# Batch 2's projections ahead of batch 0's values, and batch 3's row statistics on ScalarE

## The reference, cut to what matters

```
x [4,512,512], ctx [4,512,256]
q = ctx @ Wq.T + bq ; k = ctx @ Wk.T + bk          # [512,128] each
attention = softmax(q @ k.T, axis=-1)              # [512,512]
x1 = x + layernorm(x) @ attention.T                # x_m[l,m] = sum_n ln(x)[l,n] attention[m,n]
v  = layernorm(x1)
h  = bf16(layernorm(bf16(v)) * ln_w + ln_b)
h  = bf16(quant(h) @ quant(W1).T + b1)             # quant: 8 bits, one exponent for 32 values
h  = bf16(gelu(h))
h  = bf16(quant(h) @ quant(W2).T + b2)
out = x1 + bf16(bf16(v) + h)
```

## Time and profile before

| what | value |
|---|---|
| median of 3 runs | 273.33 us (271.74 to 273.48) |
| the profiled execution's own time | 274.33 us |
| its span, first to last instruction | 272.5 us |
| mean granted TensorE clock | 0.948 of full speed |
| DVE busy | 243.0 us, 89% of the span |
| PE busy | 226.3 us, 83% |
| ACT busy | 175.7 us, 64% |
| POOL busy | 68.1 us, 25% |
| DMA | 42.92 MB, mean 157 GB/s |

### The profile page before, as it was taken

One profiled execution on the slowest core, in us unless ns is written; L12 is line 12 of the kernel. 1 busy time (PEld: TensorE's weight loads), 2 busy tenths in 40 slices (PEclk: granted clock), 3 DMA queues, 4 the chain that ended last, 5 costly groups with the idle time before them and its releaser, 6 DMA issues.

```text
span 272.5 us, 3187 instructions
## 1 busy us (share of the span) xinstructions
PE 226.3 (83%) x931; PEld 97.5 (36%) x940; DVE 243.0 (89%) x354; ACT 175.7 (64%) x303; POOL 68.1 (25%) x101
## 2 busy tenths in 40 slices
PE   6774859989995937559996797899999789999993
PEld 6432314434431413214442333344444234444431
DVE  3599964999999999999979999999999999877982
ACT  2377753669997739767789798855556554556510
POOL 2193200042007300160521200633203333333400
PEclk9996868999999986968999999999999999999999
DMA  5999999999899828693060522656650566655773
GB/s 153 373 400 291 247 163 265 285 224 224 161 262 224 165 40 219 128 195 78 0 117 0 96 49 50 110 122 135 135 132 20 119 135 140 135 129 118 157 183 123
DMA packets 103078, 42.92 MB, mean 157 GB/s; under 512 B 93845, under 2 KB 96153, under 8 KB 102553
## 3 DMA queue, kind: packets, MB, share of 16 engines
q1 hardware_dynamic: 100224, 36.45, 61.0%
q10 hardware_dynamic: 2360, 6.30, 7.5%
q0 software_dynamic: 480, 0.02, 0.1%
HBM read 15.48 MB, written 4.19 MB: 72 GB/s over the span
## 4 chain that ended last, share of the span: by engine, by line
DVE 50%; PE 24%; DMA 10%; ACT 7%; issue 3%; SPq 3%; POOL 2%; ACTq 0%; DVEq 0%; POOLq 0%
DVE amax L862 12%; PE ps L821 9%; PE ps L811 5%; PE ps L758 5%; DMA pT<-phl 4%; DVE pf L976 4%; DVE wquant L966 4%; DVE w_int L905 3%; DVE phl L1047 3%; DMA xhl<-pf 3%; DVE vw L1059 3%; DVE hq L1064 3%; DVE xhl L1052 3%; DVE wquant L971 2%; DVE nmax L1033 2%
## 5 line engine op out<-in xcount | busy, mean ns | idle before, releaser
L821 PE MATMUL ps<-w2T,xhl 128*128 128x512 bf16 x247 | 56.5, 379 | 8.3 <-DMA xhl<-pf 7.9
L811 PE MATMUL ps<-w1T,cxT 128*128 128x512 bf16 x256 | 58.0, 380 | 0.0
L641 ACT ACTIVATE wst<-ps 128x1024 bf16<-128x1024 f32 x32 | 32.0, 1017 | 24.3 <-PE ps L811 24.3
L862 DVE TENSOR_REDUCE amax<-phl 128x64 f32<-128x2048 bf16 x16 | 36.5, 2281 | 4.0 <-ACT phl L648 4.0
L821 PEld LDWEIGHTS ps<-w2T,xhl 128*128 128x128 bf16 x256 | 24.4, 98 | 39.0 <-DMA xhl<-pf 8.3
L811 PEld LDWEIGHTS ps<-w1T,cxT 128*128 128x128 bf16 x256 | 23.7, 98 | 32.6 <-issue 6.2
L758 PE MATMUL ps<-h1q,xT 128*128 128x512 f16 x96 | 26.5, 435 | 9.8 <-ACT xs L546 6.2
L648 ACT ACTIVATE phl<-wst 128x2048 bf16<-128x2048 bf16 x16 | 30.6, 1910 | 1.6 <-DVE wquant L966 0.5
L758 PE MATMUL ps<-pT,xT 128*128 128x512 f16 x96 | 24.5, 410 | 7.5 <-DMA pT<-phl 7.0
L471 POOL TENSOR_TENSOR wst<-wst,vs 128x512 bf16<-128x512 bf16 x12 | 15.3, 1275 | 53.2 <-DVE wquant L971 53.2
L506 ACT ACTIVATE pf<-ps,nmax 128x512 f32<-128x512 f32 x16 | 10.8, 678 | 19.5 <-DVE nmax L1033 19.4
(11 more groups left out here) (90 smaller groups left out, 370.6 us busy)
## 6 DMA issues: line engine op xcount, KB each, us to landing
wst<-in_L_ffn_W ACTq DMA_DIRECT2D x6, 1024.0 KB, 6.5
xs<-in_x SPq DMA_DIRECT2D x4, 1024.0 KB, 8.0
out_x<-wst SPq DMA_DIRECT2D x16, 256.0 KB, 2.9
cx<-in_ctx SPq DMA_DIRECT2D x4, 512.0 KB, 5.7
wst<-in_L_ffn_W SPq DMA_DIRECT2D x2, 1024.0 KB, 11.3
xhl<-pf SPq DMA_TRANSPOSE x17, 4.3
lnw<-in_L_ffn_ln_w SPq DMA_DIRECT2D x1, 256.0 KB, 12.6
lnb<-in_L_ffn_ln_b SPq DMA_DIRECT2D x1, 256.0 KB, 12.2
```

Source lines behind the costliest of these rows:

```text
L641: act.activation(ys[:, k, 1024 * g:1024 * g + 1024], ps_y[:, 2 * g:2 * g + 2, :], ACT.Copy)\
L811: last = pe.matmul(ps_y[:, c, :], h1T[:, k, t, :], w1T[:, 4 * c:4 * c + 4, t, :], start=False, stop=(t == KT - 1))
L821: last = pe.matmul(ps_z[:, k, :], h2T[:, k, t, :], w2T[:, t, :], start=False, stop=(t == FT - 1))
L862: dve.tensor_reduce(amax[:, a, :], by_block, AX_X, ALU.max, apply_absolute_value=True)\
```

## The change

Five edits:

1. **SP**: the loads of `lnw` and `lnb` move from before `load_ctx(2)` to behind `front(1, 3)`, and the wait for them on DVE moves from before `front(2, ...)` to behind it, just before their first use in `back(2, 2, 0)`.
2. **PE**: a new `first_batches()` has 22 small matmuls on the identity behind `energies(0,3)` (their result is never read); `context(2)` moves before `energies(1,0)`; `queries_keys(2)` and `energies(1,2)` move ahead of `values(0,0)`; `energies(1,3)` moves before `values(0,1)`; `energies(2,0)` and `(2,1)` move in among batch 0's values.
3. **ACT**: `context(2)` moves into the first batch; `exp(1,1)`, `x_high(1,1)` and `p_high(1,0)` move ahead of batch 2's four `x_square`; `query_key(2,0)` and `(2,1)` move ahead of `p_high(1,3)`, with a wait for `energies(1,3)`, since they overwrite `qkT`.
4. **ACT, DVE and POOL**: batch 3's statistics move from DVE (`x_stats(3)` is gone) to ACT: 4 `x_sum` between `load_w1(2)` and `x_plus(0,3)`, 4 `x_square` behind `x1_square(0,3)`. POOL gets `mean_x(3)` ahead of `mean_x1(0)` and `factors_x_summed(3)` in place of `factors_x(3)`.
5. The bookkeeping counts of `st` and `mvr` lose their `min(b, 2)`.

```diff
             sp.dma_start(wst[:, W2, :], w2_t[0]).then_inc(ld_w2, 16)
-            sp.dma_start(lnw[:, :], ln_w.rearrange("(o n) -> o n", o=1).broadcast_to([P, H])).then_inc(ld_ln, 16)
-            sp.dma_start(lnb[:, :], ln_b.rearrange("(o n) -> o n", o=1).broadcast_to([P, H])).then_inc(ld_ln, 16)
             load_ctx(2)
             front(0)
             load_x(3)
             front(1, 3)
+            sp.dma_start(lnw[:, :], ln_w.rearrange("(o n) -> o n", o=1).broadcast_to([P, H])).then_inc(ld_ln, 16)
+            sp.dma_start(lnb[:, :], ln_b.rearrange("(o n) -> o n", o=1).broadcast_to([P, H])).then_inc(ld_ln, 16)
             front(2)
...
             def batch(b, x, v):
+                if b == 0:
+                    mean_x(3)
                 mean_x1(b)
                 if v is not None:
                     factors_v(v)
-                if x == 2:
+                if x is not None:
                     factors_x_summed(x)
-                elif x is not None:
-                    factors_x(x)
                 factors_x1(b)
...
+            def first_batch():
...
+                act.wait_ge(w_first, 1)
+                load_w1(1)
+                x_sum(2, 0)
+                x_sum(2, 1)
+                query_key(1, 0)
+                x_sum(2, 2)
+                query_key(1, 1)
+                context(2)
+                x_sum(2, 3)
+                exp(1, 0)
+                x_high(1, 0)
+                exp(1, 1)
+                x_high(1, 1)
+                p_high(1, 0)
+                for t in range(LT):
+                    x_square(2, t)
...
+                    if b == 0 and t == 3:
+                        act.wait_ge(e_ps, 2 * NT)
+                        query_key(2, 0)
+                        query_key(2, 1)
+                    if b > 0 and qk is not None and t == 3:
                         context(qk)
-                if front + 1 < B and b is not None:
+                if front + 1 < B:
                     load_w1(front + 1)
...
+                if b == 0:
+                    for t in range(LT):
+                        x_sum(3, t)
+                x_plus(b, LT - 1)
...
+                x1_square(b, 3)
+                if b == 0:
+                    for t in range(LT):
+                        x_square(3, t)
...
+            def first_batches():
+
+                energies(0, 2)
+                energies(0, 3)
+                keep_busy(22)
+                queries_keys(1)
+                context(2)
+                energies(1, 0)
+                energies(1, 1)
+                queries_keys(2)
+                energies(1, 2)
+                values(0, 0)
+                energies(1, 3)
+                values(0, 1)
+                values(0, 2)
+                energies(2, 0)
+                values(0, 3)
+                energies(2, 1)
...
             front(1, 1, 0, None, None)
             back(1, 1, None)
+            front(2, 2, 1, None, None)
             dve.wait_ge(ld_ln, 32)
-            front(2, 2, 1, 3, None)
             back(2, 2, 0)
```

More of the change, by code:

```diff
@@ L573, in v_sums @@
                                accum_out=sums[:, 1, 0, t:t + 1]).then_inc(v_sum, 1)
+            def first_batch():
+                for t in range(LT + 1):
+                    if t < NT:
+                        exp(0, t)
+                        x_high(0, t)
+                    if t > 0:
+                        p_high(0, t - 1)
+                    if t == 3:
+                        context(1)
+                act.wait_ge(w_first, 1)
[14 more added lines that the diff above has]
+                    x_square(2, t)
             def batch(b, front, qk, v):
                 for t in range(LT + 1):
-                    if t < NT and (t > 0 or front == 0):
+                    if t < NT and t > int(b == 0):
                         exp(front, t)
                         x_high(front, t)
-                    if t > 0:
+                    if t > int(b == 0):
                         p_high(front, t - 1)
-                    if b is not None and t > 1:
+                    if t > 1:
                         x_plus(b, t - 2)
@@ L630, in _ @@
             query_key(0, 1)
-            batch(None, 0, 1, None)
+            first_batch()
             batch(0, 1, 2, None)
@@ L764, in batch @@
             def batch(b, front, qk):
-                if qk is not None and b is not None:
+                if qk is not None:
                     context(qk)
                 for t in range(LT):
-                    if b == 0:
-                        values(b, t)
                     if t < NT - 2:
                         energies(front, t + 2)
-                    if b is not None and b > 0:
-                        values(b, t)
+                    values(b, t)
                 if qk is not None:
```

37 lines of the change are left out of this document (9 added, 28 removed).

## The result

| | before | after |
|---|---|---|
| median | 273.26 us (4 runs, 271.74 to 273.48) | 284.17 us (4 runs, 279.75 to 285.27) |
| the profiled execution, its span | 274.33, 272.5 us | 284.52, 282.7 us |
| DVE busy, and not busy, in the span | 243.0, 29.5 us | 240.2, 42.5 us |

The ratio is 1.0324, interval [1.0182, 1.0466]: slower by over 1 per cent, where 269.2 us and "faster" were forecast. The span grew by 10.2 us: DVE has 2.8 us less to do (the statistics have gone) and is idle for 13.0 us more.

A forecast was written before the change was run, and what follows sets the result against it. DVE, busy 243.0 of 272.5 us, was taken as the bound, with a 5.2 us stall on PE and ACT full behind it. 5.9 - 3.4 + 1.6 = 4.1 us less than 273.33 gave 269.2 us, range 267.3 to 271.5.

The forecast's parts named there:

- the sum: Whole kernel: 5.9 (stall gone) - 3.4 (ACT's added work) + 1.6 (statistics off DVE) = 4.1 us less.
- The paragraph on the clock: PE at full clock for `values(0,0)`, at half from about 56 us; `values(1,0)` then takes 6.1 us instead of 3.5.
- Rival E: Slower, up to 275.1 us, if crowded DMA engines start `values(0,0)` after 39.8 us at half clock; chance 0.05.
- Part 1: DVE's 5.2 us wait for `energies(1,2)` from PE goes; `negmax(1,2)` comes 5.9 us earlier, at 38.6.
- Part 2: ACT's longer row after `load_w1(2)` brings `exp(2,1)` only 2.5 us earlier; 3.4 of the 5.9 us are given back.
- Part 3: DVE drops `x_stats(3)`, 2.66 us, of which 1.6 count; `negmax(3,0)` starts 4.1 us earlier, at 83.05.
- rival B: Late transposes and half clock delay PE's `values(1,0)`, and with it `negmax(3,0)`: 3.0 us less, 270.3 us; chance 0.15.
- Rival C: Half clock at PE's `values(0,0)` makes `energies(1,3)` 1.5 us late: 2.6 us less, 270.7 us; chance 0.07.

The follow-up runs named there:

- x and context early: The changed kernel with batch 3's loads of x and context issued behind batch 0's transposes and ahead of W1's, `load_w2(1)` left in ACT's ring: 270.81 us.
- the two kernels with 1 MB more: The kernel before plus a spare 1 MB load that nobody reads, issued by ACT or by SP: 286.1 and 285.25 us.
- order only: The change without edits 4 and 5, so batch 3's statistics stay on DVE: 280.7 us (272.7 to 285.3).

## Why the prediction was wrong

**The step that failed** is not in the sum but in what the sum assumed: that each transfer lands as long after its issue as before. The paragraph on the clock says "now issued at 51.6, so 58.4 if the DMA engines keep up". Rival E says of crowding that "Nothing in the change adds to them before that", and was given 0.05 and at most 1.8 us; it looks only at the time before `values(0,0)`, and the crawl begins behind it, at 47 us. Both look at how much is moved; no byte was added, and the time between issues was what changed. The prediction moved `load_w1(2)` forward and has no line on `load_w2(1)`, which went 5.8 us forward among SP's loads and transposes. The runs show in its place: `load_w2(1)` landed in 19.0 us instead of 6.8 and the transposes in 20.0 to 24.0, DVE waited 14.3 us for weights, and the kernel came out 10.9 us slower; with that overlap taken out (273.38), or with the crawl absent for another reason (270.4 to 270.8), the loss is gone.

The Trainium skill (DMA: Bandwidth & Descriptors, Rules for kernel authors) says that a "transpose next to ordinary DMAs needs nothing". That row is about wrong results, and of time it says nothing. For the time it isn't so here: with one transpose beside a load, each took 15.5 us, instead of 3 to 8.

The rest can be judged on the change with x and context early, which is the change without the crawl:

| step | forecast | there |
|---|---|---|
| Part 1, `negmax(1,2)`, `negmax(1,3)` | 38.6, 43.0 | 38.48, 42.87 |
| Part 2, `load_w1(2)`, `exp(2,1)` | 50.8, 61.6 | 50.67, 61.61 |
| Part 2, `p_low(2,0)` | 63.6 | 63.63 |
| clock, `values(1,0)` at half clock | from 58.4 | from 61.30, 5.04 us for its 12 matmuls |
| Part 3, `negmax(3,0)` | 83.05 | 83.78, waits 1.57 for PE |
| the sum | 4.1 us | 3.3 us of span, 3.5 us of median |

- **Part 1 was right** in time and in mechanism. Its small matmuls were not needed: without them `queries_keys(1)` runs at half clock, and DVE's `negmax(1,2)` is no later.
- **Part 2 was right** to 0.1 us. The 3.4 us that ACT pays are the statistics: without these, `exp(2,1)` comes at 57.86 in the kernel with x and context early, 3.75 us before the 61.61.
- **Part 3 was 0.7 us too hopeful**, for rival B's reason. Its 1.6 us of gain stand beside a cost of 3.4 in Part 2 that belongs to the same move, so by the prediction's own terms the statistics lose 1.8 us and should have stayed on DVE. The runs show 0 to 2 us lost in the new order and 4.0 in the old, where 2.66 us of DVE's work went and 5.8 us of waits came.
- **Rival B came in** inside the kernel without the crawl: `values(1,0)` late and at half clock, `negmax(3,0)` 3.3 us early, 3.0 forecast. That its 3.3 us of span also lie near the forecast's 4.1 is no merit of the forecast, whose transposes land at 58.4.
- **Rival C didn't**: `values(0,0)` ran at full clock, 2.75 us. The granted clock fell later: in the changed kernel it is 1.00 up to 57 us and 0.50 from 58 on, with PE idle since the end of `context(3)`'s transposes at 54.1. What the Trainium skill (TensorE: Matmul & The Clock Gate, Part 4: PE-mode transpose) says of transposes, that they don't count as busy in the same way, agrees with that, but an idle PE accounts for it as well, and no run here tells the two apart.

**What stays open** is what in the DMA engines makes the crawl. The packet records of the trace show its form: from 48 to 57 us the transposes' 256-byte packets, 18 to 20 ns each otherwise, take up to some 650 ns (one 978), the load's 8 KB packets 316 ns and up to 6.9 us, and in a microsecond 3 to 8 long and 13 to 138 short ones start, where up to 48 long or 1,150 short ones do otherwise. Without the crawl the two kinds run in turns of some microseconds, each at its full rate. Why a load that starts beside a running transpose sometimes passes it as a block (at 44, 50 and 54 us in three kernels) and sometimes mixes with it (at 47 and 49, and at 53 in the two kernels with 1 MB more), I can't tell from these runs. So each cure is shown to work in its kernel, and a rule that says beforehand which order crawls is not.

## What to carry to other kernels

When a change moves work earlier, list the DMAs that move with it, by their different amounts, and ask which now overlap: here one load in one ring and transposes in another, each fine by itself, took about three times their time together. Look at GB/s beside the DMA share, not at the share alone; in the changed kernel a share of 1.20 stood beside 253 GB/s and, 4 us later, beside 79. And cost a move of work from one engine to another as one sum, what it gives less what it takes, in the new order.

## What the runs showed of the hardware that I had not expected

- A plain load of 1 MB and DMA transposes in two rings can hold each other up: landing 6.3 us apart, 15.5 beside one transpose, 19.0 with more of them behind, and 79 GB/s in place of 256 over 11 us.
- The cure is order, not less work: the load in the transposes' own ring and behind one of them (-13 us), 1 MB of x issued ahead of W1's transpose rather than behind it (-14), or a wait that keeps them apart (-11).
- It scatters. One kernel (order only) had runs 12.5 us apart (272.7 to 285.3), so a single run of such a kernel says little.
- ACT's queue issues a DMA ahead of activations in front of it: moved four activations down the program, the load was issued 0.9 us later, 1.6 us before the last of the four began.
